# Transformer block kernel on one core: new arithmetic for the reciprocal roots, work moved between engines, and a new written-out order

## The chip, the cores and the metric

The kernel runs on one core of a Trainium2 chip. A core has five engines with a queue of instructions each: PE (TensorE, matmuls and transposes), DVE (VectorE), ACT (ScalarE, activations and copies), POOL (GpSimd) and SP (SyncE, which here only issues DMAs). Each works its queue in the order in which the program was written; they meet through semaphores. The metric is the device time of one execution in microseconds (us): before the change a median of 1589.48 us over 3 runs, 1585.47 to 1590.97.

## The reference, cut to what matters

The input is x, 16 sequences of 512 tokens with 128 features. After a layer norm, two branches are computed and added to x: a full attention over heads (in which, for one token, the 16 heads of width 8 attend to one another), and two layers of a local transformer.

```python
x = L0_attn_x
xn = layernorm(x)
x = x + attn(xn, Wq, bq, Wk, bk, Wv, bv, Wo, bo) + ffn(xn, wqkv, q_scale, k_scale, wo, ln_g, ln_b, w1, b1, w2, b2)

def _layer(x, ...):                       # ffn is two of these, on the same tokens
    h = shift_token(x)                    # upper 64 features come from the token before
    q, k, v = split(h @ wqkv)             # 8 heads of 64
    q, k = l2norm(q) * qs, l2norm(k) * ksc
    q, k = rotary_xpos(q, k)
    o = local_attention(q, k, v)          # windows of 64 tokens, each looks at itself and the one before
    x = x + o @ wo
    h = shift_token(x)
    h = (h - mean) / sqrt(var + 1e-5) * lg + lb
    a, g = split(h @ w1 + b1)             # 341 hidden features each
    return x + (a * gelu(g)) @ w2 + b2
```

All arithmetic is fp32; products that need full accuracy are written as three passes over a high and a low part.

## The kernel before, in words

The work is cut into 32 **units**, one for each sequence s (0 to 15) and layer l (0 or 1); the text writes (s, l). A unit holds 512 tokens in four blocks n of 128. The full attention of a sequence (steps qkv_bias, product, full_scores, full_exp, full_values, heads) runs beside its units and is joined at the down projection of (s, 1).

One unit goes through these steps: shift_x (DMA), project_qk, square (ACT, L529), ssq (DVE sums of squares), rope (DVE, L699 and L704), rope_add (POOL, L477), rnorm (POOL, L481 and L483: maximum with a tiny number, then power -0.5), normed (POOL, L489: q and k times the reciprocal norm), qk_t (PE transposes), q_copy and k_copy (ACT), scores (PE, L845), row_max (DVE, L715), exp (ACT, L552, with a bias column and an accumulated sum), row_recip, scale (ACT, L559), probs_t (PE, L855), p_copy, values (PE, L866), o_copy, out_local (PE, L875: 8 matmuls of 512 columns), x2. Then the second norm, held feature-major (features on the partitions): center (PE, L884), center_sq (ACT, one copy and L573), variance (PE, L889), veps (DVE, L733), rstd2 (POOL, L492 and L496), spread (PE, L895), normed2 (DVE, L737), high2 and low2. Then up (PE), gelu (ACT, L583), hid (DVE, L746: gate product), down (PE, L913), and x1 with x1_split (ACT: two copies) and x1_low for layer 0, or result, final (PE transposes), add_x and store for layer 1.

What sets the order is no scheduler but tables of numbers. `all_steps` gives every step a place in time (a slot, with 50 for the distance of two units) and sorts by it; every engine then walks the same sorted list STEPS and emits its own steps. A unit (s, 0) stands at 2s, (s, 1) at 2s + 3. The next unit of a sequence, (s, 1), needs the x1_low of (s, 0).

```python
return sorted(at, key=lambda step: (at[step], step))
```

PSUM has five banks in a ring, given out by the same order (`Ring`); small tiles have two to four buffers.

Of the kernel before, what the change touches and what calls it, by code (L numbers as in the profile page):

```python
# [39 lines left out]
def spaced(first, gap, n):  # L40
    return tuple(first + gap * k for k in range(n))
# [3 lines left out]
    "shift_x": (-3.82,), "project_qk": (0.00, 14.11, 28.76, 38.54), "square": (6.11, 19.33, 31.74, 42.22),  # L45
    "rope": (10.74, 25.21, 36.75, 46.03), "ssq": (13.97, 21.89, 42.12, 47.81), "rope_add": (16.33, 30.85, 43.48, 54.20),
    "rnorm": (25.85, 29.42, 50.23, 57.09), "normed": (27.11, 36.02, 53.31, 57.43), "project_v": (31.85, 48.36, 54.05, 59.20),
    "v_copy": (32.37, 50.15, 57.53, 59.48), "move_v": (45.36, 53.43, 78.65, 80.90), "qk_t": (27.43, 40.33, 55.01, 66.39),
    "q_copy": (29.89, 43.15, 55.55, 67.09), "k_copy": (28.67, 43.54, 55.78, 67.23), "scores": (32.84, 43.61, 56.58, 73.25),
    "row_max": (36.85, 37.33, 46.97, 46.99, 58.74, 59.95, 73.67, 75.62),  # L50
    "exp": (39.37, 41.47, 47.53, 54.77, 59.95, 60.91, 75.58, 79.23),
    "row_recip": (42.15, 45.74, 49.19, 58.72, 65.29, 65.31, 77.05, 85.28),
    "scale": (44.51, 45.79, 56.16, 65.40, 72.54, 74.18, 78.54, 85.41),
    "probs_t": (45.09, 52.98, 61.43, 72.72, 74.47, 80.19, 83.38, 87.28),
    "p_copy": (47.04, 55.54, 62.54, 75.60, 78.30, 80.86, 86.05, 88.07), "values": (60.73, 81.17, 86.44, 88.63),
    "o_copy": (64.22, 83.44, 89.58, 90.23), "out_local": (91.88,), "x2": (96.57,), "shift_x2": (98.83,), "center": (103.57,),
    "center_sq": (105.11,), "variance": (105.60,), "veps": (106.19,), "rstd2": (111.36,), "spread": (111.48,),
    "normed2": (112.58,), "high2": (114.09,), "low2": (114.68,), "up": (117.10, 118.01, 119.93),
    "gelu": (118.57, 119.21, 120.28), "hid": (119.91, 121.01, 122.39), "down": (126.94,),
# [918 lines left out]
```

## Time and profile before

| | |
|---|---|
| runs | 1585.47, 1590.97, 1589.48 us; median 1589.48 |
| profiled execution | 1592.92 us, its span from first to last instruction 1590.9 us |
| busy share of the span | PE 90%, DVE 88%, ACT 90%, POOL 84% |
| granted TensorE clock, mean | 0.968 |
| HBM | 16 GB/s over the span |

Busy means that an instruction of the engine was running; shares are over the whole span, with its beginning and end, so the stages have to be looked at one by one. Durations are those of one execution. Instructions of an engine overlap a little, so what one costs its queue is the distance from its start to the start of the next, which is shorter than its own duration.

### The profile page before, as it was taken

Reading aid. Unit: us, or ns where it says so; the run is one execution under the profiler, and the core shown is the slowest. Engines: PE = TensorE matmul, PEld = TensorE weight load, DVE = VectorE, ACT = ScalarE, POOL = GpSimd, SP = SyncE. Lnnn points to the kernel's source line nnn. Section 1 sums busy time; section 2 is a strip of 40 time slices with the busy share of each in tenths; the row PEclk is TensorE's granted clock in tenths of the full one; section 3 lists DMA queues with packets and bytes.
Section 4 is the critical chain, followed back from the end, with each engine's and each line's share of the span. In section 5 each row is a group of like instructions: output and inputs, shape, how many; then the busy total and the mean of one; then the engine's idle time right before and its main releaser. Section 6 shows DMA issues by size and latency. Waiting matters only on the chain.

```text
span 1590.9 us, 37325 instructions
## 1 busy us (share of the span) xinstructions
PE 1427.8 (90%) x13496; PEld 1006.2 (63%) x13496; DVE 1405.8 (88%) x2052; ACT 1430.6 (90%) x4432; POOL 1336.1 (84%) x713
## 2 busy tenths in 40 slices
PE   1767899999999999999999999999999999999775
PEld 1545667667666666667666666667666666666453
DVE  4879999999999999999999999999999999997331
ACT  1455999999999999999999999999999999999481
POOL 2838999999999999999999999999999999996340
PEclk9778999999999999999999999999999999999797
DMA  5021313132322212232322312232322222231110
GB/s 153 16 40 25 65 35 59 41 64 54 68 54 50 55 39 56 46 67 55 67 48 50 60 40 55 47 68 55 68 43 48 60 45 54 43 68 33 42 25 26
DMA packets 206849, 82.91 MB, mean 52 GB/s; under 512 B 143266, under 2 KB 185676, under 8 KB 206668
## 3 DMA queue, kind: packets, MB, share of 16 engines
q1 hardware_dynamic: 205372, 79.97, 23.8%
q8 instruction: 109, 1.79, 0.5%
q10 hardware_dynamic: 1296, 0.56, 0.1%
q14 instruction: 72, 0.59, 0.1%
HBM read 17.60 MB, written 8.39 MB: 16 GB/s over the span
## 4 chain that ended last, share of the span: by engine, by line
PE 46%; ACT 34%; issue 7%; DVE 7%; POOL 3%; DMA 2%; ACTq 0%; SPq 0%; POOLq 0%; DVEq 0%
ACT sb_pl L552 7%; ACT sb_pl L559 7%; PE banks L875 6%; PE banks L771 5%; PE banks L845 4%; PE banks L772 4%; PE banks L773 4%; PE banks L866 4%; PE banks L855 4%; ACT sb_gate L583 4%; PE banks L831 4%; ACT sb_pT L502 3%; PE banks L913 3%; ACT sb_sq L529 2%; PE banks L839 2%
## 5 line engine op out<-in xcount | busy, mean ns | idle before, releaser
L483 POOL TENSOR_TENSOR sb_rn<-sb_rn,sb_half 128x16 f32<-128x16 f32 x128 | 374.3, 2924 | 10.7
L552 ACT ACTIVATE sb_pl<-banks,sb_nml 128x128 f32<-128x128 f32 x1024 | 371.6, 426 | 5.7 <-DVE sb_nml L715 5.7
L477 POOL TENSOR_TENSOR sb_qk<-sb_qk,sb_t 128x1024 f32<-128x1024 f32 x128 | 306.0, 2391 | 57.7 <-DVE sb_t L704 57.6
L559 ACT ACTIVATE sb_pl<-sb_pl,sb_rl 128x128 f32<-128x128 f32 x1024 | 331.9, 465 | 3.2 <-DVE sb_rl L720 3.2
L472 POOL TENSOR_TENSOR sb_pr<-sb_qkvf 128x2048 f32<-128x2048 f32 x64 | 293.1, 4579 | 32.9 <-DVE sb_qkvf L662 27.3
L552 ACT ACTIVATION_READ_ACCUMULATOR sb_pl<-banks,sb_nml 128x1 f32 x1024 | 270.8, 267 | 0.0
L489 POOL TENSOR_TENSOR sb_qk<-sb_qk,sb_rn 128x1024 f32<-128x1024 f32 x128 | 243.8, 1905 | 15.0
L771 PE MATMUL banks<-sb_wqh,sb_hh 128*128 128x512 f32 x384 | 185.0, 482 | 21.7 <-DVE sb_t L704 16.5
L855 PE MATMUL banks<-sb_ident,sb_pl 128*128 128x128 f32 x1024 | 165.4, 285 | 19.4 <-ACT sb_pl L559 9.5
L715 DVE TENSOR_REDUCE sb_nml<-banks 128x4 f32<-128x512 f32 x256 | 166.5, 682 | 17.6 <-PE banks L845 17.5
L529 ACT ACTIVATE sb_sq<-banks 128x1024 f32<-128x1024 f32 x128 | 138.4, 1081 | 43.1 <-PE banks L773 42.4
L502 ACT ACTIVATE sb_pT<-banks 128x512 f32<-128x512 f32 x256 | 163.7, 657 | 3.6 <-PE banks L855 2.6
L704 DVE TENSOR_TENSOR sb_t<-banks,sb_tab 128x512 f32<-128x512 f32 x256 | 163.6, 680 | 0.0
L699 DVE TENSOR_TENSOR sb_qk<-banks,sb_tab 128x1024 f32<-128x1024 f32 x128 | 155.1, 1212 | 5.4 <-ACT sb_sq L529 5.3
L772 PE MATMUL banks<-sb_wql,sb_hh 128*128 128x512 f32 x384 | 155.6, 405 | 0.0
L712 DVE TENSOR_REDUCE sb_ssq<-sb_sq 128x16 f32<-128x1024 f32 x128 | 155.0, 1211 | 0.4
L773 PE MATMUL banks<-sb_wqh,sb_hl 128*128 128x512 f32 x384 | 154.9, 404 | 0.0
L831 PE MATMUL banks<-sb_ident,sb_qk 128*128 128x128 f32 x1024 | 137.8, 277 | 18.6 <-ACT sb_pl L552 11.4
L866 PE MATMUL banks<-sb_pT,sb_vs 128*64 128x64 f32 x2048 | 136.9, 232 | 19.3 <-ACT sb_pT L502 19.3
L855 PEld LDWEIGHTS banks<-sb_ident,sb_pl 128*128 128x128 f32 x1024 | 116.4, 142 | 54.8 <-issue 22.8
L831 PEld LDWEIGHTS banks<-sb_ident,sb_qk 128*128 128x128 f32 x1024 | 116.3, 142 | 54.6 <-issue 34.5
L681 DVE TENSOR_REDUCE banks<-sb_pr 128x128 f32<-128x2048 f32 x64 | 146.1, 2283 | 0.0
...
## 6 DMA issues: line engine op xcount, KB each, us to landing
sb_vs<-sb_v SPq DMA_DIRECT2D x224, 128.0 KB, 2.4
...
```

Source lines behind the costliest of these rows:

```text
L472: nc.gpsimd.tensor_tensor(pr[:].rearrange("p (q k d) -> p q k d", q=H, k=H), q[:, :, None, :].to_broadcast([P, H, H, D]), k[:, None, :, :] ...
L477: nc.gpsimd.tensor_tensor(qk[:, k, :], qk[:, k, :], t2[:], ALU.add).then_inc(s_add.sem, 1)
L483: nc.gpsimd.tensor_tensor(rn[:, k, :], rn[:, k, :], half[:, 0:1].to_broadcast([P, 16]), ALU.pow).then_inc(s_rn.sem, 1)
L489: nc.gpsimd.tensor_tensor(q3, q3, rn[:, k, :, None].to_broadcast([P, 16, LD]), ALU.mult).then_inc(s_nrm.sem, 1)
L502: return nc.scalar.activation(dst, src, ACT.Copy)
L552: last = nc.scalar.activation(pl[:, k, m, :], ps[:, m * P:(m + 1) * P], ACT.Exp, bias=nml[:, k, m:m + 1], accum_out=suml[:, k, m:m + 1])
L559: last = nc.scalar.activation(pl[:, k, m, :], pl[:, k, m, :], ACT.Copy, scale=rl[:, k, m:m + 1])
L771: mm(dst, ah, bh, start=True, stop=False)
L772: mm(dst, ah, bl, start=False, stop=False)
L773: return mm(dst, al, bh, start=False, stop=True)
L831: last = nc.tensor.transpose(ps[:, a * P:(a + 1) * P], qk[:, TURN[step] % 2, k * 512 + a * P:k * 512 + (a + 1) * P], ident[:])
L855: last = nc.tensor.transpose(ps[:, k * P:(k + 1) * P], pl[:, TURN[step] % PLS, k, :], ident[:])
```

## The change

It does the following.

- rnorm takes two blocks at once, 128x32 numbers, and twelve small POOL operations (a bit-trick seed and two refinement steps) stand in place of one maximum and one power.
- The norm of q is no longer multiplied into q: normed handles k alone (512 columns), row_max writes the raw maxima, a new POOL step row_scale multiplies them with the norms (128x8), and exp takes the norm as a scale column beside its bias column.
- Blocks of odd n of scale move from ACT to POOL. The gate product hid moves from DVE to POOL, with a new ACT step up_copy in front of it, since POOL doesn't read PSUM.
- The second norm is token-major: shift_x2 (three DMAs), stats2 (DVE), rstd2 (POOL), norm2 (ACT, like the first norm), norm2_t (PE transposes); center, center_sq, variance, veps, spread and normed2 are gone. x1 and x2 are token-major as well: out_local and down swap their operands, so each 512-column matmul becomes four of 128 columns; x1_t (PE transposes) is new, and final is gone. The biases b2 and bo are rows of the down weights.
- sq, t2, ob have two buffers, qk, xt, x1 and the scratch in memory three, ssq and rn four.
- All slots are new, and the first and last units and full attentions have places of their own.

```diff
-LAYER_AT = (0.0, 3 * PERIOD)
-FIRST_LATER, LAST_SOONER = 1.13, 6.33
+LAST_UNITS = ((B - 2, 0), (B - 1, 0), (B - 3, 1), (B - 2, 1), (B - 1, 1))
+LAST_AT = (-5.0134, -3.5342, -2.5699, -1.0860, -0.1123)
+HEADS_AT = (1.4193, 2.0653, 3.8098, -4.8828, -1.3446)
...
+def unit_at(s, l):
+    if (s, l) in FIRST_UNITS:
+        return FIRST_AT[FIRST_UNITS.index((s, l))]
+    if (s, l) in LAST_UNITS:
+        return 2 * B + LAST_AT[LAST_UNITS.index((s, l))]
+    return 2 * s + (2 if l else -1)
...
+            def newton(op, x, y):
+                tt, ts = nc.gpsimd.tensor_tensor, nc.gpsimd.tensor_scalar
+                if op == 0:
+                    return ts(hx_, x, TINY, 0.5, ALU.max, ALU.mult)
+                if op == 1:
+                    return ts(y.bitcast(I32), hx_.bitcast(I32), -0.5, SEED, ALU.mult, ALU.add)
+                if op in (2, 8):
+                    return tt(hxy_, hx_, y, ALU.mult)
...
                 if kind == "rnorm":
-                    nc.gpsimd.tensor_scalar(rn[:, k, :], ssq[:, k, :], TINY, None, ALU.max).then_inc(s_rn.sem, 1)
-                    nc.gpsimd.tensor_tensor(rn[:, k, :], rn[:, k, :], half[:, 0:1].to_broadcast([P, 16]), ALU.pow).then_inc(s_rn.sem, 1)
+                    for op in range(12):
+                        if op:
+                            pool.wait_ge(s_rn.sem, s_rn.at(step, step, op))
+                        newton(op, x, y).then_inc(s_rn.sem, 1)
...
+                if kind == "hid":
+                    pool.wait_ge(s_upc.sem, s_upc.at(same("up_copy", step, n), step))
+                    pool.wait_ge(s_gelu.sem, s_gelu.at(same("gelu", step, n), step))
+                    nc.gpsimd.tensor_tensor(hid[rows, n, :], hid[rows, n, :], gate[rows, TURN[step] % 2, :], ALU.mult).then_inc(s_hid.sem, 1)
+                if kind == "row_scale":
+                    nc.gpsimd.tensor_tensor(nml[:, k:k + 2, :], nmx[:, 2 * TURN[step] % 4:2 * TURN[step] % 4 + 2, :],
+                                            rn[:, TURN[step] % RNS, 0:LH].rearrange("p (a h) -> p h a", h=2), ALU.mult).then_inc(s_nml.sem, 1)
+                if kind == "scale" and n in POOL_SCALED:
+                    nc.gpsimd.tensor_tensor(pl[:, k, :, :], pl[:, k, :, :], rl[:, k, :, None].to_broadcast([P, 4, P]), ALU.mult).then_inc(s_scale[1].sem, 1)
...
                 if kind == "exp":
-                    act.wait_ge(s_max.sem, s_max.at(same("row_max", step, n), step))
+                    act.wait_ge(s_nml.sem, s_nml.at(same("row_scale", step, n // 2), step))
...
-                                                    bias=nml[:, k, m:m + 1], accum_out=suml[:, k, m:m + 1])
+                                                    scale=rn[:, TURN[step] // 2 % RNS, 2 * m + n % 2:2 * m + n % 2 + 1], accum_out=suml[:, k, m:m + 1])
...
-                    copy(hc[:], ps)
-                    nc.scalar.activation(sq2[:], ps, ACT.Square).then_inc(s_csq.sem, 1)
+                if kind == "norm2":
+                    for b in range(NB):
+                        last = nc.scalar.activation(hn[:, b, :], hs[:, b, :], ACT.Identity, bias=nmr2[:, b:b + 1], scale=rs2[:, b:b + 1])
...
+                if kind == "up_copy":
+                    nc.scalar.activation(hid[rows, n, :], bank(same("up", step, n), 1)[rows, :], ACT.Identity, bias=b1[rows, l, 0, n:n + 1]).then_inc(s_upc.sem, 1)
...
-                    for a in range(NPAIR):
-                        last = mm(ps, wo_local[:, l, a, :], oTl[:, a, :], start=a == 0, stop=a == NPAIR - 1)
+                    for b in range(NB):
+                        o = slice(b * P, (b + 1) * P)
+                        for a in range(NPAIR):
+                            last = mm(ps[:, o], oTl[:, a, o], wo_local[:, l, a, :], start=a == 0, stop=a == NPAIR - 1)
```

The order at two places. First ACT near the end of the program, around the last row that writes sb_sh, which is the x1_split of (15, 0): with it (15, 0) is done and the last unit (15, 1) can begin. Before:

```order
L502 ACTIVATE sb_x<-banks 128x512
L502 ACTIVATE sb_sh<-banks 128x512
L502 ACTIVATE sb_pT<-banks 128x512
L502 ACTIVATE sb_oTl<-banks 128x4x128 x2
L529 ACTIVATE sb_sq<-banks 128x1024
L502 ACTIVATE sb_hc<-banks 128x512
L573 ACTIVATE sb_sq<-banks 128x512
L529 ACTIVATE sb_sq<-banks 128x1024
L502 ACTIVATE sb_mh<-banks 128x512
L583 ACT_TABLE_LOAD
```

The same place on ACT after the change (L577 copies, L601 squares, L624 exp, L645 norm2):

```order
L577 ACTIVATE sb_oTl<-banks 128x4x128
L577 ACTIVATE sb_sh<-banks 128x512
L577 ACTIVATE sb_oTl<-banks 128x4x128
L577 ACTIVATE sb_oT<-banks 128x512
L601 ACTIVATE sb_sq<-banks 128x1024
L577 ACTIVATE sb_qT<-banks 128x512
L577 ACTIVATE sb_kT<-banks 128x4x128
L601 ACTIVATE sb_sq<-banks 128x1024
L577 ACTIVATE sb_qT<-banks 128x512
L577 ACTIVATE sb_kT<-banks 128x4x128
L624 ACTIVATE sb_pl,sb_suml<-banks,sb_nml,sb_rn 128x128 x4
L645 ACTIVATE sb_hn<-sb_hs,sb_nmr,sb_rs 128x128 x4
```

Exps and a norm2 of (13, 1) and (14, 1) now stand behind that point. Counted to the end of the program, ACT had behind it 32 copies of 512 columns, 4 squares of 1024 columns, 32 exps, 32 scales, 2 squares of 512 columns and 6 gelus; it now has 55 such copies, 6 squares, 64 exps, 32 scales, 12 norm2, 9 gelus, 9 up_copies and 2 full_exps. Table loads are 3 in both.

Second, POOL in the middle of the program, one stretch around the second norm. Before (L477 rope_add, L481 and L483 rnorm, L489 normed, L492 and L496 rstd2, L472 product):

```order
L477 TENSOR_TENSOR sb_qk<-sb_qk,sb_t 128x1024
L481 TENSOR_SCALAR sb_rn<-sb_ssq 128x16
L483 TENSOR_TENSOR sb_rn<-sb_rn,sb_half 128x16
L489 TENSOR_TENSOR sb_qk<-sb_qk,sb_rn 128x1024
L492 TENSOR_TENSOR sb_rsq<-sb_veps,sb_half 128x4
L496 TENSOR_TENSOR sb_sq<-sb_ident,sb_rsq 128x512
L472 TENSOR_TENSOR sb_pr<-sb_qkvf 128x2048
```

After (the end of a rnorm, then L562 scale, L547 normed, L552 hid, L534 rope_add):

```order
L509 TENSOR_SCALAR sb_aux<-sb_aux 128x32
L510 TENSOR_TENSOR sb_rn<-sb_rn,sb_aux 128x32
L562 TENSOR_TENSOR sb_pl<-sb_pl,sb_rl 128x512
L547 TENSOR_TENSOR sb_qk<-sb_qk,sb_rn 128x512
L552 TENSOR_TENSOR sb_hid<-sb_hid,sb_gate 128x512
L534 TENSOR_TENSOR sb_qk<-sb_qk,sb_t 128x1024
L547 TENSOR_TENSOR sb_qk<-sb_qk,sb_rn 128x512
L552 TENSOR_TENSOR sb_hid<-sb_hid,sb_gate 128x512
L552 TENSOR_TENSOR sb_hid<-sb_hid,sb_gate 85x512
L562 TENSOR_TENSOR sb_pl<-sb_pl,sb_rl 128x512
```

The scaling and the gate product of other units now stand between the steps that feed the transposes of q and k.

## Rows read from the trace of the kernel before

**Rows 1.** Windows: busy of PE, PEld, DVE, ACT, POOL; clock, DMA share, GB/s.
```profile
400.00:800.00 400.00, 381.74 (x3745) 270.24 (x3747) 382.00 (x559) 396.18 (x1233) 370.52 (x195) 1.00 0.26 55
...
1481.15:1590.90 109.75, 76.95 (x500) 49.32 (x500) 32.67 (x51) 50.87 (x145) 33.73 (x20) 0.79 0.14 34
```
**Rows 2.** Timeline of ACT (start, length in us): table loads of two gelus, 24 units apart.
```profile
300.46 1.28 ACT L583 ACT_TABLE_LOAD   x1
...
1379.02 1.28 ACT L583 ACT_TABLE_LOAD   x1
```
**Rows 3.** Timeline of ACT: norm, copy, two exps with their accumulator read between.
```profile
679.35 1.76 ACT L512 ACTIVATE sb_xt<-sb_xt,sb_nmr,sb_rs 128x128 f32<-128x128 f32 x4
680.89 0.71 ACT L502 ACTIVATE sb_pT<-banks 128x512 f32<-128x512 f32 x1
681.37 0.49 ACT L552 ACTIVATE sb_pl<-banks,sb_nml 128x128 f32<-128x128 f32 x1
...
681.71 0.49 ACT L552 ACTIVATE sb_pl<-banks,sb_nml 128x128 f32<-128x128 f32 x1
```
**Rows 4.** Timeline of ACT: scales and their successor, gelus, a square, a gelu.
```profile
820.36 2.47 ACT L559 ACTIVATE sb_pl<-sb_pl,sb_rl 128x128 f32<-128x128 f32 x8
822.70 0.41 ACT L596 ACTIVATE banks<-banks 128x256 f32<-128x256 f32 x1
...
841.37 1.27 ACT L583 ACTIVATE sb_gate<-banks,sb_b 128x512 f32<-128x512 f32 x2
842.53 1.03 ACT L529 ACTIVATE sb_sq<-banks 128x1024 f32<-128x1024 f32 x1
843.44 0.69 ACT L583 ACTIVATE sb_gate<-banks,sb_b 128x512 f32<-128x512 f32 x1
```
**Rows 5.** Timeline of POOL in the middle of the run.
```profile
832.61 1.04 POOL L496 TENSOR_TENSOR sb_sq<-sb_ident,sb_rsq 128x512 f32<-128x512 f32 x1
833.61 4.57 POOL L472 TENSOR_TENSOR sb_pr<-sb_qkvf 128x2048 f32<-128x2048 f32 x1
...
838.56 0.23 POOL L462 TENSOR_SCALAR sb_ve<-sb_mv 128x4 f32<-128x4 f32 x1
838.87 1.04 POOL L464 TENSOR_TENSOR sb_rs<-sb_ve,sb_half 128x4 f32<-128x4 f32 x1
839.98 0.20 POOL L466 TENSOR_TENSOR sb_nmr<-sb_nmr,sb_rs 128x4 f32<-128x4 f32 x1
840.13 2.40 POOL L477 TENSOR_TENSOR sb_qk<-sb_qk,sb_t 128x1024 f32<-128x1024 f32 x1
842.62 0.26 POOL L481 TENSOR_SCALAR sb_rn<-sb_ssq 128x16 f32<-128x16 f32 x1
842.96 2.92 POOL L483 TENSOR_TENSOR sb_rn<-sb_rn,sb_half 128x16 f32<-128x16 f32 x1
846.02 1.90 POOL L489 TENSOR_TENSOR sb_qk<-sb_qk,sb_rn 128x1024 f32<-128x1024 f32 x1
```
**Rows 6.** Timeline of PE: out_local and its successor, variance and its successor.
```profile
817.44 3.60 PE L875 MATMUL banks<-sb_oTl,sb_wo_local 128*128 128x512 f32 x8
820.88 0.59 PE L839 MATMUL banks<-sb_mask,sb_identb 128*128 128x512 bf16 x2
...
829.41 0.95 PE L889 MATMUL banks<-sb_mean_of,sb_sq 128*128 128x1 f32 x8
830.22 0.59 PE L839 MATMUL banks<-sb_mask,sb_identb 128*128 128x512 bf16 x2
```
**Rows 7.** Groups by line and shape: busy us, mean ns, idle before.
```profile
L746 DVE SCALAR_TENSOR_TENSOR sb_hid<-banks,sb_b,sb_gate 128x512 f32<-128x512 f32 x96 | 69.1, 745 | 15.0 <-ACT sb_gate L583 11.6 <-PE banks L773 3.3
L875 PEld LDWEIGHTS banks<-sb_oTl,sb_wo_local 128*128 128x128 f32 x256 | 48.5, 200 | 57.8 <-issue 51.6 <-ACT sb_oTl L502 6.2
```
**Rows 8.** Timeline of DVE: x_low of (15, 0), and its x1_low.
```profile
1353.46 0.68 DVE L658 TENSOR_TENSOR sb_sl<-banks,sb_sh 128x512 fp32r<-128x512 f32 x1
...
1481.86 0.69 DVE L755 TENSOR_TENSOR sb_sl<-banks,sb_sh 128x512 fp32r<-128x512 f32 x1 [3.41 <-ACT sb_sh L502]
```

More of the change, by code:

```diff
@@ L23 @@
 EPS = 1e-5
+SEED = float(0x5f3759df - (1 << 22))
 TINY = 1e-24
-MASKED = -2.0 ** 124
+MASKED = -2.0 ** 80
 SCALE = float(D) ** -0.5
 ND = 2 * NB
-PLS = 4
+PLS, RNS = 4, 4
+POOL_SCALED = (1, 3, 5, 7)
+QKB = 3
 PERIOD = 50.0
-LAYER_AT = (0.0, 3 * PERIOD)
-FIRST_LATER, LAST_SOONER = 1.13, 6.33
-def spaced(first, gap, n):
-    return tuple(first + gap * k for k in range(n))
-UNIT_SLOTS = {
[L45 to L59, printed above, removed]
@@ L154, in released_by @@
     last = {"fold": "biases", "norm_t": "x_low", "qkv_full": "qkv_bias", "project_v": "v_copy", "qk_t": ("q_copy", "k_copy")[k], "scores": "exp",
-            "probs_t": "p_copy", "values": "o_copy", "out_local": "x2", "center": "center_sq", "variance": "veps", "spread": "low2",
-            "up": ("gelu", "hid")[k], "down": ("x1_low", "result")[l], "attn_t": "o_t", "final": "add_x"}[kind]
+            "probs_t": "p_copy", "values": "o_copy", "out_local": "x2", "norm2_t": "low2", "x1_t": "x1_low",
+            "up": ("gelu", "up_copy")[k], "down": ("x1", "add_x")[l], "attn_t": "o_t"}[kind]
     return last, s, l, 2 * n + k if kind == "scores" else n
@@ L309, in build @@
         s_x2 = signal("x2_done", "x2")
-        s_hs = signal("x2_shifted", "shift_x2", unit=32)
-        s_cen = signal("centred", "center")
-        s_csq = signal("centred_squares", "center_sq")
-        s_var = signal("variance_filled", "variance")
-        s_veps = signal("variance_copied", "veps")
-        s_rs2 = signal("mlp_rstd_steps", "rstd2", 2)
-        s_spread = signal("rstd_spread", "spread")
-        s_n2 = signal("mlp_normed", "normed2")
+        s_hs = signal("x2_shifted", "shift_x2", unit=48)
+        s_bn2 = signal("mlp_block_stats", "stats2")
+        s_st2 = signal("mlp_stats", "stats2")
+        s_rs2 = signal("mlp_rstd_steps", "rstd2", 3)
+        s_n2 = signal("mlp_normed", "norm2")
+        s_n2t = signal("mlp_transposed", "norm2_t")
         s_h2 = signal("mlp_high", "high2")
@@ L487, in _ @@
                     pool.wait_ge(s_add.sem, s_add.at(same("rope_add", step, n), step))
[L488 to L492 removed]
+                    pool.wait_ge(s_rn.sem, s_rn.at(same("rnorm", step, n // 2), step))
@@ L511, in _ @@
                     for b in range(NB):
-                        last = nc.scalar.activation(xt[:, b, :], xt[:, b, :], ACT.Identity, bias=nmr[:, b:b + 1], scale=rs4[:, b:b + 1])
+                        last = nc.scalar.activation(xt[:, s % 3, b, :], xt[:, s % 3, b, :], ACT.Identity, bias=nmr[:, b:b + 1], scale=rs4[:, b:b + 1])
                     last.then_inc(s_norm.sem, 1)
@@ L734, in _ @@
[L734 to L737 removed]
+                    nc.vector.tensor_tensor(x2[:, k, :, :], blocks(bank(same("out_local", step, 0))), residual, ALU.add).then_inc(s_x2.sem, 1)
+                if kind == "stats2":
+                    dve.wait_ge(s_hs.sem, s_hs.at(same("shift_x2", step, 0), step))
+                    for b in range(NB):
+                        last = nc.vector.bn_stats(st2[:, b, :], hs[:, b, :])
+                    last.then_inc(s_bn2.sem, 1)
+                    dve.wait_ge(s_bn2.sem, s_bn2.at(step, step))
+                    if before(step):
+                        dve.wait_ge(s_rs2.sem, s_rs2.at(("rstd2", *before(step)[1:]), step))
+                    for b in range(NB):
+                        last = nc.vector.bn_aggr(mv2[:, b, :], st2[:, b, :])
+                    last.then_inc(s_st2.sem, 1)
```

411 lines of the change are left out of this document (224 added, 187 removed).

## The prediction

> **What bounds the kernel now.** I read the stretches first, then ACT's timeline, then the other queues. In the middle of the run ACT is busy 396.2 of 400 us, DVE 382.0, PE 381.7 and POOL 370.5, at a full clock [rows 1]. So ACT sets the pace there, with less than 1% of idle, and the others have 4 to 7% to spare. The pace: 24 units lie between two table loads at 300.46 and 1379.02, which is 44.9 us each [rows 2]. 32 times 44.9 is 1438 us; the other 153 us of the span of 1590.9 are spent at the two ends. The far end is one stretch. (15, 0) is done at 1481 and (15, 1), which needs it, runs almost alone from there: 109.75 us in which ACT is busy 50.9 [rows 1]. A change can therefore win in two places only: in ACT's work per unit, or by putting work into the ends. What it takes off DVE or PE buys at most the 0.4 us per unit that ACT now waits ((400 - 396.2) over 8.9 units).
>
> **ACT per unit.** Costs are distances from one start to the next. A group of eight scales takes 2.34 us, 0.29 each; a copy of 512 columns 0.48; an exp with its accumulator read 0.34; a norm activation, which has a scale and a bias column, 1.54/4 = 0.385 [rows 3, 4]. Two gelus take 1.16, 0.58 each, 0.10 more than the copy of the same size: that is the price of the bias column [rows 3, 4]. The norm against the scale (0.385 to 0.29) says the same of a second column: 0.09.
> - Half of scale leaves: 16 x 0.29 = -4.7.
> - Exp gets a scale column: 32 x 0.09 = +3.0. The trace shows no exp with two columns. It could be hidden behind the accumulator read (0) or cost up to 0.10 (+3.2); I take 0.09, from the nearest rows.
> - center_sq (two activations of 512) and one more copy per unit (xT or the plain x1) leave: -3 x 0.48 = -1.4.
> - norm2: 4 x 0.385 = +1.5. up_copy: 3 x 0.58 = +1.7.
>
> The sum is +0.1 us per unit, about +4.5 over 32 units with rounding upward. So the most loaded engine gets nothing, and the pace stays at 44.9.
>
> **The other queues, per unit.** POOL [rows 5]: the old rnorm takes 3.4 from its start to the next, 4 x 3.3 = 13.2 off; normed on half the columns saves 4 x (1.90 - 1.04) = 3.4. On: 24 small operations. Those of 4 to 16 columns take 0.20 to 0.26, and the next starts 0.08 after the end, since each waits for the last; at 2.1 ns a column (4.57 less 2.40 over 1024) I put 32 columns at 0.34 to 0.37, together 8.5. hid: a 512-column product of two full operands is between 1.0 and half of 2.57, 3 x 1.3 = 3.9. scale: 4 x 1.04 = 4.2, priced by L496. row_scale: 4 x 0.2 = 0.8. rstd2: about -0.2. Sum +0.6, on 41.4 busy (370.5 over 8.9): 42.0 of 44.9, not counting gaps. Bounds for the small operations: the arithmetic on bit patterns has no row; it lies between 0.20 and the 1.04 of the power on four columns, the slowest small row, and if all 24 ran 0.1 longer as well the sum would be +4 instead of +0.6. If they are as short as 0.20 with the wait, it is -1.
>
> DVE: hid leaves, 69.1/32 = -2.2 [rows 7]; normed2 and veps go and the statistics on hs come, which about cancel. It was not the bound, so I book 0.
>
> PE: the centring and the spreading matmuls, 4 x 0.43, the variance, 0.81, and the transposes of final leave, -2.7; norm2_t and x1_t bring +0.7. The swapped products are 60 pairs of 128 columns instead of 15 of 512. One of 512 takes 0.43 (3.44/8), so 128 columns take 0.107; and a pair that moves one column takes 0.10, which is what loading the weights costs a queue [rows 6]. At 0.11 a pair it is 6.6 against 6.45. PE gains 1.9 us per unit, and that too is no bound: 0.
>
> Here a rule of the Trainium skill speaks against the change. The page "TensorE: Matmul & The Clock Gate", section "The mechanism" in the part on packing, says that a weight load overlaps running matmuls only when the row group differs. These loads fill all 128 rows, so by it each of the 60 pairs would cost its load on top. The trace disagrees for full-row pairs: a weight load of L875 lasts 0.200 [rows 7], its matmul moves 512 columns, and yet pairs follow each other every 0.43, and 0.107 of streaming is a quarter of that.
>
> **The ends.** The order moves work behind the point at which (15, 1) can start, the last write of sb_sh on ACT. By the counts given with the order, ACT has behind it 23 more copies (11.0), 2 more squares (1.8, at 0.91 [rows 4]), 32 more exps (10.9) and 64 scale columns (5.8), 12 norm2 for 2 squares (3.7), 3 gelus and 9 up_copies (7.0) and 0.6 of full_exp: 41 us more, where 50.9 of 109.75 were used. That work stood ahead of the point before, when ACT was full. So (15, 1) can start up to 41 - 4.5 = 36.5 us sooner.
>
> Two things give part of it back. (15, 0) took 128.4 us from x_low to x1_low with the queues full [rows 8]; by the same count only about 107 us of ACT work now lie on its way, and a unit alone needs 110, so the unit itself becomes the limit. I take 7 us, between 0 and 20. And (15, 1) is no longer alone: its queues now hold 92 us of ACT work. Its length lies between 109.75 and the 128.4 of a unit among full queues; I take 119, +9, since ACT would be some 75% full. The chain of the unit itself changes little: norm2 spares the matmuls of center, variance and spread, while hid gets up_copy and a slower product; 0, within 3 either way. At the beginning the first unit still has little beside it; the full attention of sequence 0 is pressed closer, which loads DVE before the first gelu: 0, within 8. For the closer coupling of the queues (exp now waits for POOL, down for POOL) I add +1, between -12 (ACT's idle gone) and +30.
>
> Sum: 1590.9 - 36.5 + 7 + 9 + 1 = 1571.4 for the span. The profiled execution is 2.0 longer than its span (1592.92) and stands 3.4 above the median of 1589.48, so for the median of the runs I say **1570**. Its own range is 1552 to 1584.
>
> **The rivals.**
> - *POOL becomes the bound.* Place: the middle of the run. exp waits for row_scale, which stands in POOL's queue behind products of 4.6 us, the k norm and the twelve chained operations; and behind a waiting row_scale stand rope_add and the next rnorm, for which PE's transposes and again ACT wait. It decides once POOL's sum passes about +2.5 us per unit, or the waits cost ACT more than 1 us. For it: POOL gets about 900 instructions more and now feeds every stage. Against: the sum of +0.6. At +1.2 us a unit over 31 units: 1570 + 37 = 1607, slower than before.
> - *The ends give everything back.* (15, 1) takes the 128.4 of a unit among full queues and (15, 0) is held up by 15: 1570 + 9 + 8 = 1587, within the error of no change. For it: both units pass through in-order queues with other units' steps written between. Against: these queues are only three quarters full.
> - *The exp's second column is free*, or PE and DVE, relieved by about 2 us each, take ACT's waits with them. Then ACT's sum is -2.9 and the pace falls until the next engine binds (POOL, at 42.0 and its gaps): -1.2 us a unit, 1570 - 37 = 1533. Against: the norm's 0.385.
> - *Weight loads come out from under the matmuls.* With load and stream in a row a pair takes 0.10 + 0.107 and PE gets 60 x 0.1 = 6 us more per unit, 4 net of what leaves: its 42.9 (381.7 over 8.9) becomes 47, and with its usual gaps 49. At 4 us a unit: 1570 + 130 = 1700. By the page's rule above it is this; the trace bears it out so little that I give it 2%.
>
> **Chances.** Forecast 0.51, free column or fewer waits 0.16, POOL 0.19, ends eaten 0.12, weight loads 0.02. What a measurement of this kernel can tell from no change is about 0.3%, 4.8 us, so the same is 1584.7 to 1594.3. Faster: 0.51 + 0.16 + a third of 0.12 = 0.71. Slower: 0.19 + 0.02 - 0.02 for a mild POOL = 0.19. Same 0.10. The range that leaves out 2 in 10 reaches to 1533 below and 1607 above.
>
> **What the profile after would show.** In the middle: ACT still at 99%, DVE and PE at 90 to 93%, POOL at 93 to 96%, and 44.5 to 45.2 us between units; exp plus read at 0.43 from start to start; a rnorm of twelve in 4.1 to 4.4; a pair of out_local every 0.11. At the end: the last sb_sh near 1450 and 115 to 125 us behind it with ACT busy over 85. I would be wrong in the place if the pace is off 44.9 by more than 0.5, or if ACT's idle names POOL (sb_nml, sb_hid) as what it waited for; and wrong in the size if the last stretch is 109 or 135 long.

## The result, and the profile after

The changed kernel takes 1748.71 us (median of 4 runs, 1747.23 to 1750.68), the kernel before beside it 1587.76. The ratio is 1.1013, with an interval of 1.0988 to 1.1038: 10% slower, 179 us above the forecast of 1570 and outside its range. Of the profiled execution the page says (busy us, share, instructions; then the chain that ended last):

```profile
span 1746.6 us, 40282 instructions
PE 1430.4 (82%) x14680; PEld 1149.1 (66%) x14680; DVE 1347.3 (77%) x2148; ACT 1446.5 (83%) x4046; POOL 1269.3 (73%) x1639
ACT 31%; PE 21%; DVE 19%; SPq 15%; issue 7%; DMA 5%; POOL 3%; DVEq 0%; ACTq 0%; POOLq 0%
```

No engine has much more to do than before, and none is full: in the windows that answer to [rows 1], ACT, once busy 396 of 400 us, is busy 364. The order of columns is as there; the second row is the last stretch, from the x1_low of (15, 0) on, now 146.3 us instead of 109.75.

```profile
400.00:800.00 400.00, 352.78 (x3686) 285.46 (x3686) 334.23 (x535) 363.57 (x1023) 317.58 (x410) 0.94 0.23 49
1600.30:1746.60 146.30, 96.96 (x949) 76.83 (x947) 60.97 (x110) 90.10 (x253) 64.52 (x88) 0.85 0.16 36
```

What is new is SP's queue in the chain, with 15%. Its timeline in one unit (start, length of the issue), and the two engines behind it:

```profile
802.17 0.66 DVE L812 TENSOR_TENSOR sb_x<-banks,sb_xt 128x512 f32<-128x512 f32 x1
802.86 0.76 SPq L470 DMA_DIRECT2D sb_hs<-sb_x  x1
803.66 6.55 SPq L471 DMA_DIRECT2D sb_hs<-sb_x  x1
810.25 0.68 SPq L472 DMA_DIRECT2D sb_hs<-sb_x  x1
812.68 0.87 DVE L816 BATCH_NORM_STATS2 sb_st<-sb_hs 128x6 f32<-128x128 f32 x4 [6.08 <-DMA sb_hs<-sb_x]
814.06 0.24 POOL L567 TENSOR_SCALAR sb_nmr<-sb_mv 128x4 f32<-128x4 f32 x1 [6.02 <-DVE sb_mv L822]
```

L470 to L472 are the three DMAs of shift_x2. The issue of the second holds SP for 6.55 us (6.44 to 6.55 in all 32 units), the others for 0.7. x2 is written at 802.8, stats2 can begin at 812.7, and DVE stood still for 6.08 us before it. It is tempting, and wrong, to blame L471: it moves one partition, 0.8 KB. The windows of this stretch (last three columns: clock, share of the 16 DMA engines, GB/s) show who is really at work:

```profile
804.00:806.00 2.00, 1.94 (x36) 1.62 (x37) 2.00 (x5) 2.00 (x6) 2.00 (x1) 1.00 0.09 21
806.00:808.00 2.00, 2.00 (x18) 1.63 (x16) 0.60 (x2) 1.95 (x5) 2.00 (x2) 1.00 0.08 18
808.00:810.00 2.00, 1.90 (x36) 1.35 (x36) 0.00 (x0) 2.00 (x9) 0.04 (x1) 1.00 0.08 18
```

The rate is a flat 18 GB/s at a share of 0.08, close to one engine of sixteen (0.06), for 6 to 7 us, and that is the size of L470, 127 KB. The packets in the trace say the same: those of 256 bytes start one every 14 ns from 804.3 to 811.6, one behind the other, and L470 has 508 of them (in split_112_15 below 508 such packets start within 1.2 us). So L470, whose 127 partitions all go through one DMA engine, is the suspect, and L471 the one that waits. The Trainium skill has the rule ("DMA: Bandwidth & Descriptors", section "Why a DMA increments its semaphore by 16 and not by 1"): the number of DMA engines is the largest one up to 16 that divides the slowest dimension, so 127 partitions go through one. The trace agrees, with these 14 ns and the share of 0.08.

How the late norm becomes time is in the waits of the middle, 400 to 1200 us (total, times, longest):

```profile
DVE sb_st L816 <- DMA sb_hs<-sb_x: 89.2, 16, 6.1
ACT sb_hn L645 <- POOL sb_nmr L572: 38.7, 16, 2.9
PE banks L947 <- ACT sb_v L577: 72.3, 16, 5.0
```

DVE waits for sb_hs; ACT, which walks its list in order, stands 2.4 us a time in front of norm2 for the statistics from rstd2; and PE stands 4.5 us a time in front of values, since v_copy is behind norm2 on ACT. After these waits the granted clock falls as well: it is 0.94 in the middle, where it was 1.00.

To measure the pace over the same units in every kernel I take ACT's copy to sb_mh (high2), one per unit: the 7th and the 27th. Before and after:

```profile
432.06 0.72 ACT L502 ACTIVATE sb_mh<-banks 128x512 fp32r<-128x512 f32 x1
...
1330.93 0.79 ACT L502 ACTIVATE sb_mh<-banks 128x512 fp32r<-128x512 f32 x1
```
```profile
473.48 0.60 ACT L577 ACTIVATE sb_mh<-banks 128x512 fp32r<-128x512 f32 x1 [0.81 <-PE banks L964]
...
1466.22 0.60 ACT L577 ACTIVATE sb_mh<-banks 128x512 fp32r<-128x512 f32 x1
```

The pace is (1330.93 - 432.06) / 20 = 44.94 before and (1466.22 - 473.48) / 20 = 49.64 after. Of the 156 us of span that were added, 41 are lost in the first seven units, 94 in these twenty, 20 behind them.

### The profile page after: what moved, and what is told of

It is laid out like the page before. It is cut to its first block, busy times and chain, and to the rows that moved or that the text cites. A ratio compares the mean times of both kernels' runs of the same rounds, so it can differ in the third digit from the quotient of the medians.

```text
span 1746.6 us, 40282 instructions
## 1 busy us (share of the span) xinstructions
PE 1430.4 (82%) x14680; PEld 1149.1 (66%) x14680; DVE 1347.3 (77%) x2148; ACT 1446.5 (83%) x4046; POOL 1269.3 (73%) x1639
## 4 chain that ended last, share of the span: by engine, by line
ACT 31%; PE 21%; DVE 19%; SPq 15%; issue 7%; DMA 5%; POOL 3%; DVEq 0%; ACTq 0%; POOLq 0%
SPq L471 12%; ACT sb_pl L624 9%; DMA sb_hs<-sb_x 4%; ACT sb_pl L631 4%; PE banks L947 3%; DVE banks L748 3%; DVE sb_ssq L794 3%; ACT sb_hid L662 3%; PE banks L851 3%; PE banks L925 3%; ACT sb_gate L657 2%; PE banks L988 2%; ACT L657 2%; PE banks L852 2%; PE banks L853 2%
## 5 line engine op out<-in xcount | busy, mean ns | idle before, releaser
L624 ACT ACTIVATE sb_pl<-banks,sb_nml,sb_rn 128x128 f32<-128x128 f32 x1024 | 455.7, 478 | 13.5 <-POOL sb_nml L557 13.4
L534 POOL TENSOR_TENSOR sb_qk<-sb_qk,sb_t 128x1024 f32<-128x1024 f32 x128 | 302.9, 2366 | 13.8 <-DVE sb_t L784 13.8
L624 ACT ACTIVATION_READ_ACCUMULATOR sb_pl<-banks,sb_nml,sb_rn 128x1 f32 x1024 | 231.4, 226 | 0.0
L947 PEld LDWEIGHTS banks<-sb_pT,sb_vs 128*64 128x64 f32 x2048 | 115.7, 152 | 147.6 <-ACT sb_v L577 112.3
L799 DVE TENSOR_REDUCE sb_nmx<-banks 128x4 f32<-128x512 f32 x256 | 163.7, 680 | 56.7 <-PE banks L925 56.7
L601 ACT ACTIVATE sb_sq<-banks 128x1024 f32<-128x1024 f32 x128 | 134.2, 1049 | 56.5 <-PE banks L853 56.0
L816 DVE BATCH_NORM_STATS2 sb_st<-sb_hs 128x6 f32<-128x128 f32 x128 | 27.9, 281 | 184.6 <-DMA sb_hs<-sb_x 184.6
L936 PE MATMUL banks<-sb_ident,sb_pl 128*128 128x128 f32 x1024 | 149.2, 282 | 22.4 <-ACT sb_pl L631 10.1
L631 ACT ACTIVATE sb_pl<-sb_pl,sb_rl 128x128 f32<-128x128 f32 x512 | 165.2, 416 | 1.8 <-DVE sb_rl L804 1.8
L562 POOL TENSOR_TENSOR sb_pl<-sb_pl,sb_rl 128x512 f32<-128x512 f32 x128 | 133.8, 1045 | 33.6 <-DVE sb_rl L804 33.4
L577 ACT ACTIVATE sb_pT<-banks 128x512 f32<-128x512 f32 x256 | 149.3, 616 | 7.1 <-PE banks L936 5.4
L911 PE MATMUL banks<-sb_ident,sb_qk 128*128 128x128 f32 x1024 | 140.1, 281 | 15.1 <-POOL sb_qk L547 15.1
L552 POOL TENSOR_TENSOR sb_hid<-sb_hid,sb_gate 128x512 f32<-128x512 f32 (+1 forms) x96 | 121.9, 1284 | 39.7 <-ACT sb_hid L662 34.0
```

Of the source, the lines that this page charges most:

```text
L534: nc.gpsimd.tensor_tensor(qk[:, k, :], qk[:, k, :], t2[:, TURN[step] % 2, :], ALU.add).then_inc(s_add.sem, 1)
L624: last = nc.scalar.activation(pl[:, k, m, :], ps[:, m * P:(m + 1) * P], ACT.Exp, bias=nml[:, k, m:m + 1], scale=rn[:, TURN[step] // 2 % RN ...
L631: last = nc.scalar.activation(pl[:, k, m, :], pl[:, k, m, :], ACT.Copy, scale=rl[:, k, m:m + 1])
L799: nc.vector.tensor_reduce(nmx[:, k + h, :], bank(same("scores", step, n), h).rearrange("p (a b) -> p a b", a=4), AX_X, ALU.max, negate=Tru ...
L947: last = mm(ps[h * LD:(h + 1) * LD, pair * P + w * WIN:pair * P + (w + 1) * WIN], vals[:, n, head * LD:(head + 1) * LD], pT[:, turn, pair, ...
```

## The experiments

### Which DMA, and what it hurts

Three kernels tell the form of L471 from the 127 partitions of L470. **split_112_15:**

```diff
-sp.dma_start(hs[1:P, :, 64:128], x2[0:P - 1, k, :, 64:128])
+sp.dma_start(hs[1:113, :, 64:128], x2[0:112, k, :, 64:128])
+sp.dma_start(hs[113:P, :, 64:128], x2[112:P - 1, k, :, 64:128])
```


> The changed kernel with the first DMA of shift_x2 cut in two, 112 partitions and 15, instead of 127 in one. Nothing else changes; the DMA of one partition behind it (L471 in the changed kernel, whose issue takes 6.5 us there) stays. Theory A (127 rows go through one DMA engine, and the next issue on SP's queue waits for it): the issue of the one-partition DMA falls from 6.5 us to under 1, sb_hs lands 5 us sooner, and the time falls from 1748 to 1540 to 1600, where my sum put it. Rival B (a DMA of one partition is itself slow to issue): its issue stays at 6.5 us and the time stays within 10 us of 1748. Rival C (the SP queue's time is hidden, the loss is POOL's new place in front of exp): the issue gets short and the time stays over 1680.

1627.45 us, ratio 1.0252 (1.0235 to 1.0269): 121 us sooner, though above what theory A gave. The one-partition DMA is L472 here (duration min/median/max in ns):

```profile
L470 SPq DMA_DIRECT2D sb_hs<-sb_x x32: 657/663/749, 121.8 to 1594.7; - x32
L471 SPq DMA_DIRECT2D sb_hs<-sb_x x32: 937/942/972, 122.6 to 1595.4; - x32
L472 SPq DMA_DIRECT2D sb_hs<-sb_x x32: 739/747/751, 123.6 to 1596.4; - x32
```

**no_edge:** L471 taken out.

> The changed kernel without the one-partition DMA of shift_x2: the upper half of the features of tokens 128, 256 and 384 of every sequence is left out of the shifted x2 and stays zero. Theory A (the 127-row DMA blocks the queue): the 6.5 us move to the issue of the next DMA (the lower 64 features, 128 partitions), which takes 6 to 7 us instead of 0.68, and the time stays within 15 us of 1748. Rival B (the one-partition form is slow): all other issues stay under 0.8 us and the time falls by 100 us or more, to under 1650.

1740.53 us, ratio 1.0970 (1.0948 to 1.0993). The 6.5 us have moved to the issue that now stands behind the 127 partitions, the 128-partition DMA of the lower features that took 0.68 before:

```profile
L470 SPq DMA_DIRECT2D sb_hs<-sb_x x32: 716/722/815, 121.0 to 1702.0; - x32
L471 SPq DMA_DIRECT2D sb_hs<-sb_x x32: 6410/6458/6532, 121.9 to 1702.7; - x32
```

**rows127_last:** L470 behind L472.

> The changed kernel with the three DMAs of shift_x2 in another order: one partition, then the lower 64 features, then the 127 rows last. Theory A: the one-partition issue falls under 1 us, and the issue behind the 127 rows, whichever DMA that is (move_v, store, heads), takes up to 6.5 us if it comes at once. The landing of sb_hs comes about 1.5 us sooner, so the time falls a little, by 0 to 60 us, and stays over 1680. Rival B: the one-partition issue stays at 6.5 us in its new place and the time is within 15 us of 1748.

1775.87 us, ratio 1.1188 (1.1171 to 1.1206). All three issues are under 0.8 us and the long ones are those of move_v and store behind. In its time both stories missed: it got slower, by 27 us. The 127 rows start 1.5 us later and land last; from the end of x2 to stats2 it is 10.8 us instead of 9.8 (medians of 32 units), and the pace is 50.52 instead of 49.64. That pointed to latency rather than to the blocked queue, so two kernels put the same DMA into the kernel before, with a spare target in memory. **before_127**, behind the two DMAs of shift_x2; **before_127_first**, ahead of them and counted with them:

```diff
 sp.dma_start(hs[64:128, 1:S], x2[64:128, k, 0:S - 1]).then_inc(s_hs.sem, 16)
+sp.dma_start(spare[1:P, :, :], wo_local[0:P - 1, 0, :, 64:128]).then_inc(s_spare.sem, 16)
```
```diff
+sp.dma_start(spare[1:P, :, :], wo_local[0:P - 1, 0, :, 64:128]).then_inc(s_hs.sem, 16)
 sp.dma_start(hs[0:64, :], x2[0:64, k, :]).then_inc(s_hs.sem, 16)
```


> The kernel before with one more DMA per unit behind the two of shift_x2: 127 partitions of 4 x 64 numbers from a weight tile to a spare tensor in memory, for which nothing waits except the next one of its own. It adds the blocking of SP's queue alone, not the latency of the norm. Theory A: the issue of the DMA behind it takes 5 to 7 us and the time rises, by 10 to 100 us, as far as move_v, shift_x and heads stand behind it and have no slack. Rival B: every issue stays under 1 us and the time stays within 5 us of 1588.

> The kernel before with the same spare DMA of 127 partitions as in before_127, but ahead of the two of shift_x2 and counted with them, so that center waits for it: latency for the second norm and blocking of the queue, where before_127 (1588 us, no change) had the blocking alone. Theory (the 6.5 us hurt as latency of the second norm, not as time of SP's queue): sb_hs lands 6 to 7 us later in each unit, center waits up to 6 us on PE, and the time rises by 60 to 170 us, to 1650 to 1760. Rival (SP's queue time, in the changed order, was what hurt, and the old order has room for a late sb_hs as well): 1583 to 1610.

before_127: 1587.96 us, ratio 1.0005 (0.9994 to 1.0016). The queue is blocked, as the issue of move_v (L416) shows, and it costs nothing:

```profile
823.27 0.69 SPq L440 DMA_DIRECT2D spare_rows_copy<-sb_wo_local  x1
825.16 5.42 SPq L416 DMA_DIRECT2D sb_vs<-sb_v  x1
830.62 0.60 SPq L418 DMA_DIRECT2D sb_vs<-sb_v  x1
```

before_127_first: 1845.08 us, ratio 1.1605 (1.1586 to 1.1624), a pace of 52.9. From x2 to center it is now 10.1 us, where the kernel before has 3.6 (medians). PE stands in front of center and the whole norm behind it (400 to 1200 us):

```profile
ACT sb_hc L504 <- PE banks L886: 112.0, 15, 7.6
PE banks L886 <- DMA sb_hs<-sb_x: 93.5, 15, 6.9
```

So the one-engine DMA costs 121 us of the changed kernel. In the kernel before, blocking alone costs nothing, and 6.5 us of latency in front of the second norm cost 8 us in each unit. That is more than their length, and the clock may be the rest: it is 0.94 instead of 1.00 in the middle, and the matmuls of center, right behind the wait, take 1.13 us instead of 0.59.

### The other 57 us

split_112_15 is still 57 us above 1570. Its milestones are 450.23 and 1368.42, a pace of 45.91; ACT's own work from 7th to 27th is 42.19 us a unit beside its table loads, 41.97 before. So 0.22 of the 0.97 is work, the rest waits. In the columns of [rows 1]:

```profile
400.00:800.00 400.00, 371.82 (x3993) 300.57 (x3994) 359.92 (x569) 388.53 (x1093) 341.74 (x447) 0.97 0.25 53
```

The further kernels are changes to split_112_15.

| kernel | edit | us | ratio (interval) | pace |
|---|---|---|---|---|
| split_scale6 | POOL_SCALED = (1, 2, 3, 5, 6, 7) | 1647.19 | 1.0388 (1.0368, 1.0407) | 46.55 |
| split_scale0 | POOL_SCALED = () | 1762.57 | 1.1109 (1.1088, 1.1129) | 50.20 |
| split_v6 | project_v, v_copy, move_v 6 slots sooner | 1638.78 | 1.0336 (1.0319, 1.0353) | 46.24 |
| no_shift | the four DMAs out, norm on x2 | 1621.89 | 1.0215 (1.0184, 1.0245) | 45.77 |
| split_x2_3 | out_local, x2, shift_x2 3 slots sooner | 1679.69 | 1.0573 (1.0546, 1.0600) | 47.96 |
| lower_dve | lower features by DVE, no fourth DMA | 1632.84 | 1.0273 (1.0254, 1.0293) | 45.84 |
| norm2_later | norm2 279.20 instead of 278.33 | 1627.12 | 1.0241 (1.0209, 1.0273) | 45.80 |
| filled_gap | see below | 1619.85 | 1.0193 (1.0168, 1.0218) | 45.56 |
| o_later | o_copy 2, 3 later by 1.5 slots | 1638.08 | 1.0311 (1.0289, 1.0333) | 46.10 |
| first_regular | first units by the rule | 1624.91 | 1.0232 (1.0208, 1.0255) | 45.73 |
| split_regular | last units by the rule | 1620.34 | 1.0216 (1.0197, 1.0234) | 45.92 |

**ACT's work.**

> The changed kernel with the 112 + 15 cut, and six instead of four of eight scale steps on POOL. Theory (ACT's own work sets the pace of 46.07 us a unit, as ACT is busy 778.7 of 800 us): ACT loses 8 x 0.29 = 2.3 us a unit, POOL gets 2 x 1.04 = 2.1 and stands at 41.5; the pace falls to 43.8 to 44.5 and the time from 1627 to 1565 to 1590. Rival (the waits between the queues set the pace: exp for row_scale, values for move_v, down for hid): the time stays within 12 us of 1627, or rises since POOL gets fuller.

> The changed kernel with the 112 + 15 cut, and all eight scale steps on ACT, as before the change. Theory (ACT's own work sets the pace): 16 x 0.29 = 4.7 us a unit come back, over 28 to 31 units 130 to 145 us: 1745 to 1775. Rival (waits set the pace): under 1690, since a relieved POOL answers row_scale sooner.

Upward the theory holds: 4.4 us more work on ACT, 4.3 more pace. Downward it fails: ACT gets 2.1 less (40.09) and the pace rises by 0.6. ACT now waits between 400 and 1200 us 20.4 us for project_v in front of v_copy, 15.1 in front of q_copy and 11.0 for row_scale in front of exp, where split_112_15 has none of these waits. So ACT is the bound only from one side; here the hand-overs of the written order are next at once. The edit also gives POOL 2.1 us a unit, and no run takes work off ACT alone, so the two aren't parted.

**The shift's latency and the place of the steps.**

> The changed kernel without the four DMAs of shift_x2 (of the 112 + 15 version): stats2 and norm2 read x2 itself, in the same places of the order. The token shift in front of the second norm is left out. It takes the whole latency of the shift (3.05 us of issues and 2.3 to land) off the second norm and 3 us per unit off SP's queue. Theory L (what is left over 44.9 us a unit is the shift's latency, since DVE still waits about 1 us for sb_hs in 13 of 17 units, and POOL, ACT and PE behind it): the pace falls from 46.1 to 44.8 to 45.2 and the time from 1627 to 1575 to 1600. Rival O (the order's hand-overs between ACT and PE set it, v_copy behind norm2 above all, whatever sb_hs does): within 10 us of 1627.

> The changed kernel with the 112 + 15 cut, and out_local, x2 and shift_x2 three slots (2.7 us) earlier in the order of every unit; stats2 and the rest of the norm stay where they are. Theory L: DVE's wait for sb_hs goes and the time falls by 15 to 45 us, to 1582 to 1612. Rival O: within 10 us of 1627, or slower, since PE's out_local now comes close behind the last o_copy and waits there.

> The changed kernel with the 112 + 15 cut, in which DVE copies the lower 64 features from x2 to sb_hs (128 x 256 numbers, 0.4 us) instead of the fourth DMA. sb_hs is complete 0.7 us sooner, DVE gets 0.4 us more a unit. Theory L: the time falls by 5 to 20 us, to 1607 to 1622. Rival O: no more than 5 us either way, or slower by the 0.4 us of DVE a unit, 13 us.

> The changed kernel with the 112 + 15 cut, and project_v, v_copy and move_v 6 slots (about 5.5 us) earlier in the order of every unit. Theory (PE's 77 us of waits in front of values are the landing of move_v behind a late v_copy, and they count, since PE's stalls lower its granted clock to 0.97 in the middle): the waits in front of values fall under 20 us, the clock rises to 0.99 or more and the time falls by 10 to 35 us, to 1592 to 1617. Rival (ACT's own work sets the pace, these waits are cover): the waits fall and the time stays within 8 us of 1627.

Without any shift the ratio is 1.0215, and its interval overlaps that of split_112_15: at 5 us of latency the norm is no longer what counts, and rival O holds. lower_dve says the same: DVE's waits for sb_hs fall from 36.9 to 5.6 us over the whole run, and the time does not fall. The two kernels that moved steps sooner became slower. In split_v6 PE's wait moved from values to norm2_t (31.4 us of 800, still for v_copy) and the clock stayed at 0.97; in split_x2_3 DVE waits 34.4 us for out_local, and ACT 15.7 for row_recip and 13.2 for row_scale. That these waits come from steps passed on the same queues is my reading of the order and was not tried.

**The gap on PE.** In split_112_15 PE stands still once in each unit, for v_copy, which on ACT is behind a square and norm2:

```profile
813.36 1.71 ACT L646 ACTIVATE sb_hn<-sb_hs,sb_nmr,sb_rs 128x128 f32<-128x128 f32 x4
814.89 1.15 ACT L578 ACTIVATE sb_v<-banks 128x512 f32<-128x512 f32 x2
```
```profile
815.61 0.34 PE L948 MATMUL banks<-sb_pT,sb_vs 128*64 128x64 f32 x4 [1.98 <-ACT sb_v L578]
```

One unit earlier the same gap ends at 769.2, and then the granted clock falls (columns as in [rows 1]; the clock is the third from the end; 0.58 is a mean of full speed and of 0.5, that is 1.2 GHz):

```profile
764.00:770.00 6.00, 4.02 (x43) 3.21 (x43) 5.93 (x8) 6.00 (x19) 5.92 (x5) 1.00 0.13 38
770.00:774.00 4.00, 3.36 (x21) 2.43 (x18) 4.00 (x8) 4.00 (x18) 3.50 (x7) 0.58 0.59 131
774.00:778.00 4.00, 4.00 (x12) 3.12 (x11) 4.00 (x4) 2.91 (x4) 3.50 (x9) 0.57 0.40 105
```

This happens in ten of the twenty units. ACT is idle for 1.1 us from 774 to 778, while PE gets through 12 matmuls in 4 us. norm2_later puts norm2 behind the v_copies, filled_gap puts useless matmuls ahead of the gap, for block 2 (`n == 2`):

```diff
-parts3(ps, hh[:, u, c], hl[:, u, c], wqh[:, l, o], wql[:, l, o]).then_inc(s_v.sem, 1)
+for again in range(3 if n == 2 else 1):
+    last = parts3(ps, hh[:, u, c], hl[:, u, c], wqh[:, l, o], wql[:, l, o])
+last.then_inc(s_v.sem, 1)
```


> The changed kernel with the 112 + 15 cut, and norm2 0.87 slots later in the order, so that on ACT it stands behind the two v_copies instead of ahead of them; PE, DVE and POOL keep their order. Theory G (in the 112 + 15 version PE stands still for 1.98 us in each unit, since values claims a bank that the v_copy behind norm2 frees; in many units the granted clock then falls to 0.5 for 3.4 to 6.8 us and ACT waits for the slower matmuls): the gap splits into two of about 1 us, the clock in the middle rises from 0.97 to 0.99 or 1.00, the pace falls from 46.1 to 45.0 to 45.5, and the time from 1627 to 1590 to 1610. Rival W (the gap is slack of an engine that isn't the bound, and the clock does no harm): within 6 us of 1627.

> The changed kernel with the 112 + 15 cut, and project_v of block 2, whose matmuls are the last of their kind ahead of the gap on PE, done three times over (the same result written again): six more matmuls of 512 columns, 6 x 0.235 = 1.4 us of PE a unit. The order is unchanged. It is work for nothing, placed where PE would stand still. Theory G: the gap shrinks from 1.98 to about 0.6 us, the clock rises to 0.99 or more in the middle, and the time falls by 10 to 35 us although PE has more to do: 1592 to 1617. Rival W (PE's own work and hand-overs, not the clock): 0 to 40 us slower, as PE gets 1.4 us a unit.

> The same with the last five units and last two full attentions at the places of the rule, as in split_regular (1620 us). Theory G: 20 to 35 us below 1620, so 1585 to 1600. Rival W: within 6 us of 1620. If the ends are worth the same here as there, it stands 4 to 10 us below norm2_later.

filled_gap: the clock is 1.00 in the middle, the pace 45.56 instead of 45.91, and the time 7.6 us less although PE has 1.4 us a unit more to do. norm2_later splits the gap (0.46 us for v_copy and 0.95 to 1.24 for norm2), the clock is 0.99, and the time is the same: 1627.12. norm2_later_regular: 1622.30, ratio 1.0207 (1.0184 to 1.0230), as split_regular without it. So in filled_gap the steady clock is worth some 0.35 us a unit, a third of what is missing, not the 1 us that theory G promised. That rests on this one kernel: norm2_later has nearly the same clock and gains nothing, and whether its later norm2 costs what the clock gives back no run shows. The middle of filled_gap:

```profile
400.00:800.00 400.00, 380.40 (x4097) 304.64 (x4101) 364.52 (x578) 393.01 (x1109) 347.27 (x450) 1.00 0.26 54
```

**The wait in front of o_copy.** ACT's own waits from 450 to 1350 us in split_112_15 (total, times, longest):

```profile
ACT sb_oTl L578 <- PE banks L948: 10.6, 30, 0.5
ACT sb_sq L602 <- PE banks L854: 6.0, 8, 1.1
```

> The changed kernel with the 112 + 15 cut, and o_copy of blocks 2 and 3 placed 1.5 slots later, so that on ACT one or two other steps go ahead of it (norm of the next sequence, exps); only ACT's order changes. In the middle ACT waits for values in front of it, 10.6 us in 900. Theory (a wait of the engine that sets the pace costs its full length): these waits go, 0.5 us a unit less, 1605 to 1618. Rival (the wait moves to the next hand-over, since x2 and the second norm come later): 1622 to 1640.

The same view of o_later:

```profile
ACT sb_sq L602 <- PE banks L854: 11.1, 24, 1.1
ACT sb_oT L578 <- PE banks L1002: 6.7, 9, 0.7
ACT sb_sh L578 <- PE banks L995: 3.1, 9, 0.3
ACT sb_oTl L578 <- PE banks L948: 0.8, 1, 0.8
```

The wait left o_copy and came back, longer in all (22.2 us instead of 19.1, with the smaller rows), in front of the squares and the copies of sb_oT and sb_sh: the rival holds.

**The ends.**

> The changed kernel with the 112 + 15 cut, and the last five units and last two full attentions at the places that the rule for the middle gives ((14,0) -5, (15,0) -3, (13,1) -4, (14,1) -2, (15,1) 0 before the end) instead of their own. Theory (the written-out end pays, by my term of -36.5 + 16): 12 to 30 us slower than 1627, so 1639 to 1657, with the last stretch nearer 110 us and thin. Rival (the ends give everything back): within 8 us of 1627.

> The changed kernel with the 112 + 15 cut, and the first five units and first three full attentions at the places of the rule ((0,0) -1, (1,0) 1, (0,1) 2, (2,0) 3, (1,1) 4; attentions at -1, 1, 3 at full length) instead of their own. Seven units of second norm are done 18 us later in the written-out beginning than in the kernel before. Theory (the squeezed beginning, DVE and POOL loaded with full attention while the weights are prepared, costs this): 5 to 18 us faster, 1609 to 1622. Rival (it is the lower clock and the longer chain of the new unit when it is alone, at any places): 1622 to 1650.

The written-out end gains nothing over the rule. The last stretches, first of split_112_15, then of split_regular:

```profile
1494.50:1625.60 131.10, 94.67 (x948) 74.94 (x946) 61.10 (x110) 89.99 (x253) 64.38 (x88) 0.89 0.19 41
```
```profile
1520.80:1620.90 100.10, 65.26 (x558) 52.69 (x554) 28.98 (x57) 51.94 (x135) 35.09 (x54) 0.81 0.13 31
```

(15, 1) begins 26.3 us sooner in the first and takes 31.0 longer; the intervals of the two ratios just miss each other (1.0234 and 1.0235), so the written-out end is worth nothing or a small loss. At the beginning, too, the rule does as well (1624.91).

**combined:** split_regular, filled_gap and o_later together.

> The changed kernel with the 112 + 15 cut, the ends of split_regular (-7 us), the filled gap (-7.6 us) and the later o_copies together. If the gains add up and o_later brings 10: 1598 to 1606. If o_later brings nothing: 1608 to 1616. It beats the kernel before (1588) only if all three add up and the waits in front of the squares go as well, which I give one chance in ten.

1629.39 us, ratio 1.0255 (1.0234 to 1.0275). With o_later's own 10.6 us of loss the three would add up to 1623.4, so the gains did not add up either, by 6 us. No version beat the kernel before.

## Why the prediction was wrong

**The step that failed** is the cost of the second norm's new form. The part on the change counted center_sq, the copy, norm2, the statistics and the matmuls, and at "The chain of the unit itself changes little" (0, within 3 either way) it priced the chain without the three DMAs of shift_x2; the old two were never set beside them. In the kernel before, center begins 3.6 us after x2 (median). Here stats2 begins 9.9 us after it (802.83 to 812.68; median 9.8), and 4.9 with 112 + 15 partitions (802.78 to 807.67; median 5.0). With it fell "the pace stays at 44.9", which took ACT's own work for all that sets the pace: ACT stands 2.4 us in each unit for this norm. By its own signs the prediction was wrong in the place: the pace is 49.6, and ACT's longest wait names POOL, though for sb_nmr and not for sb_nml or sb_hid. The 5 us, with the queue behind them, are worth 121 us of 179. Which of latency and blocking it is in the changed order, no run parts. The trace speaks for latency: from 400 to 1200 us PE waits 3.6 us in all for sb_hl, and otherwise no engine waits for any DMA but sb_hs. In the kernel before it is latency alone.

The rest, by span (1625.6 of split_112_15 against the forecast 1571.4, in all 54):

- *The pace.* "The pace stays at 44.9" was off by 0.97, which is 19 us from the 7th to the 27th unit. ACT's work went up by 0.22 where I had +0.1; waits make the rest, 0.75 a unit or 15 us over these twenty. The coupling of the queues stood in the sum with +1 and in the bounds with 30, so it was mis-sized by about 14.
- *The beginning.* Booked at 0, within 8. The 7th unit is 18 us later, and 9 of them are there at the first high2 (135.9 against 126.5 us). In first_regular, with the first units at the places of the rule, the first high2 comes at 129.0 but the 7th is still 17 us late, so the places aren't the cause; what it is stays open.
- *The end.* I had -36.5 + 7 + 9 = -20.5. Behind the 27th unit it is -3 (257.2 against 259.9). (15, 1) lasts 131.1 instead of my 119, though ACT is busy for 90.0 of it, as I had estimated (92). The step that was wrong is the estimate that a unit among queues three quarters full takes no more than 119: the rival "the ends give everything back" was right here.

**What held.** ACT's prices: an exp with scale column and its read takes 0.435 from start to start where I had 0.43.

```profile
822.11 0.46 ACT L624 ACTIVATE sb_pl<-banks,sb_nml,sb_rn 128x128 f32<-128x128 f32 x1
822.46 0.20 ACT L624 ACTIVATION_READ_ACCUMULATOR sb_pl<-banks,sb_nml,sb_rn 128x1 f32 x1
822.55 0.46 ACT L624 ACTIVATE sb_pl<-banks,sb_nml,sb_rn 128x128 f32<-128x128 f32 x1
```

POOL's: the twelve operations take 3.9 us (I had 4.1 to 4.4), the one on bit patterns no longer than its neighbours, and hid 1.28.

```profile
839.88 0.32 POOL L495 TENSOR_SCALAR sb_hx<-sb_ssq 128x32 f32<-128x32 f32 x1
840.29 0.22 POOL L497 TENSOR_SCALAR sb_rn<-sb_hx 128x32 int32<-128x32 int32 x1
840.59 0.25 POOL L499 TENSOR_TENSOR sb_hxy<-sb_hx,sb_rn 128x32 f32<-128x32 f32 x1
...
843.49 0.25 POOL L510 TENSOR_TENSOR sb_rn<-sb_rn,sb_aux 128x32 f32<-128x32 f32 x1
```

POOL never became the bound, 342 of 400 us in split_112_15. PE's swapped products: out_local takes 3.56 us for 32 pairs from its start to the next, 0.11 each as I had it, and the weight loads (0.19 us each) stayed under the matmuls, against the rule of the Trainium skill that the prediction weighed ("TensorE: Matmul & The Clock Gate", "The mechanism"):

```profile
795.97 3.81 PE L957 MATMUL banks<-sb_wo_local,sb_oTl 128*128 128x128 f32 x32
799.53 0.48 PE L851 MATMUL banks<-sb_wqh,sb_hh 128*128 128x512 f32 x1
```

What is left open: how to be rid of the 0.4 us a unit that ACT waits longer in filled_gap than in the kernel before, and the 18 us of the beginning. The trace names the 0.4: from 450 to 1350 us ACT waits 10.6 us for values in front of o_copy and 2.5 in front of the squares, where the kernel before has 6.3 in all. But split_v6, norm2_later and o_later each took a wait away and saw another come elsewhere.
